# Front slots with the softmax shift ahead of the next normalisation, both filler matmuls in one place, one more front slot, and the fp8 and gate transposes one slot later

## What is computed

```python
x = x + _L0_xattn_ref(_layernorm(x, axis=-1), ctx_1024, ...)
x = x + _L0_ffn_ref(_layernorm(x, axis=-1), ...)      # six layers of local attention
x = x + _L1_xattn_ref(_layernorm(x, axis=-1), ctx_1024, ctx_1024, ...)
x = x + _L1_ffn_ref(_layernorm(x, axis=-1), L1_ffn_weight, L1_ffn_weight_scale, L1_ffn_bias)
x = x + _L2_xattn_ref(_layernorm(x, axis=-1), ctx_1024, ctx_1024, ...)
x = x + _L2_ffn_ref(_layernorm(x, axis=-1), ...)      # shared expert + top 2 of 8
x = x + _L3_xattn_ref(_layernorm(x, axis=-1), ctx_1024, ctx_1024, ...)
x = x + _L3_ffn_ref(_layernorm(x, axis=-1), ...)      # top 2 of 8 experts
```

## Time and profile before

| | |
|---|---|
| median of 3 runs | 2570.82 us (2570.54 to 2572.94) |
| the profiled execution's own time | 2574.15 us |
| its span | 2572.4 us |
| merged part, from the first `turn_x` to the end | 1734.8 to 2572.4 us |
| of it front slots 0 to 14, to the first expert matmul | 1734.8 to 1892.2 us |
| PE, DVE, ACT, POOL busy in the span | 2402.7, 1905.8, 1463.0, 1178.8 us |

### The profile page before, as it was taken

The page is one execution under the profiler, slowest core; times in us unless marked ns, Lnnn a source line. Parts: engine busy times, 40 slices in busy tenths (PEclk is TensorE's granted clock), DMA queues, the critical chain, the costliest instruction groups (busy, mean ns, idle before and its releaser), DMA issues.

```text
span 2572.4 us, 61077 instructions
## 1 busy us (share of the span) xinstructions
PE 2402.7 (93%) x25528; PEld 1452.4 (56%) x25528; DVE 1905.8 (74%) x3472; ACT 1463.0 (57%) x2051; POOL 1178.8 (46%) x867
## 2 busy tenths in 40 slices
PE   6887899999999999999999999977789999999999
PEld 5775566665666666566666566644444455554443
DVE  4765899999899999999999989935666666454322
ACT  2332566666666666666666666623356677665443
POOL 1221777767777777777776767711111111111000
PEclk9998999999999999999999999988899999999999
DMA  3000000100000000000000100002000001021111
GB/s 120 5 5 5 1 2 2 33 4 12 18 18 7 7 26 10 7 7 26 10 13 2 34 2 10 2 1 83 7 31 14 30 16 39 28 64 50 37 38 41
DMA packets 36006, 55.95 MB, mean 22 GB/s; under 512 B 6365, under 2 KB 20710, under 8 KB 35498
## 3 DMA queue, kind: packets, MB, share of 16 engines
q1 hardware_dynamic: 35754, 52.33, 6.6%
HBM read 51.13 MB, written 1.19 MB: 20 GB/s over the span
## 4 chain that ended last, share of the span: by engine, by line
PE 52%; DVE 25%; ACT 11%; issue 9%; POOL 3%; SPq 0%; DMA 0%; DVEq 0%; POOLq 0%; ACTq 0%
PE w L1402 9%; PE w L1412 8%; DVE turned L1056 4%; DVE norm L1063 4%; PE w L765 4%; PE w L790 4%; PE w L778 4%; PE py L803 4%; PE w L519 3%; DVE straight_odd L1051 2%; DVE top L568 2%; PE w L856 2%; ACT sq L1002 2%; PE w L1531 2%; ACT sq L993 2%
## 5 line engine op out<-in xcount | busy, mean ns | idle before, releaser
L593 POOL TENSOR_TENSOR prob<-prob,rden 128x1024 f32<-128x1024 f32 x112 | 213.2, 1904 | 207.5 <-DVE rden L582 207.5
L563 ACT ACTIVATE prob<-logit 128x512 f32<-128x512 f32 x224 | 137.6, 630 | 282.2 <-DVE logit L571 282.2
L1402 PE MATMUL w<-qT,m_fc 128*128 128x512 f32 x544 | 270.3, 609 | 0.0
L1172 POOL TENSOR_TENSOR straight_odd<-straight_odd,turned 128x1024 f32<-128x1024 f32 x96 | 227.3, 2368 | 82.8 <-DVE turned L1056 79.9
L1172 POOL TENSOR_TENSOR straight<-straight,turned 128x1024 f32<-128x1024 f32 x96 | 226.5, 2368 | 45.0 <-DVE turned L1056 45.0
L1056 DVE TENSOR_TENSOR turned<-w,rot 128x512 f32<-128x512 f32 x384 | 245.6, 681 | 0.0
L1166 POOL TENSOR_TENSOR straight_odd<-straight_odd,rnorms 128x1024 f32<-128x1024 f32 x96 | 180.6, 1902 | 116.9 <-DVE rnorms L1077 116.9
L1063 DVE TENSOR_REDUCE norm<-sq 128x16 f32<-128x1024 f32 x192 | 224.3, 1211 | 0.0
L1166 POOL TENSOR_TENSOR straight<-straight,rnorms 128x1024 f32<-128x1024 f32 x96 | 180.5, 1900 | 72.4 <-DVE rnorms L1077 72.4
L611 POOL TENSOR_TENSOR fresh_roots<-fresh_means,eps 128x1 f32<-128x1 f32 x64 | 12.1, 190 | 401.2 <-DVE fresh_means L600 401.2
L765 PE MATMUL w<-b_wqkv,m_proj 128*128 128x512 f32 x384 | 192.8, 625 | 2.8 <-DVE turned L1056 1.5
(11 more groups left out here) (259 smaller groups left out, 5270.0 us busy)
## 6 DMA issues: line engine op xcount, KB each, us to landing
b_wqkv<-gates SPq DMA_DIRECT2D x64, 256.0 KB, 3.7
b_wqkv<-in_b_wqkv SPq DMA_DIRECT2D x18, 512.0 KB, 3.6
ctxT<-in_ctxT SPq DMA_DIRECT2D x64, 64.0 KB, 1.8
...
```

Of the source, the lines that this page charges most:

```text
L593: pool.tensor_tensor(flat, flat, k.rden[:, s, :, None].broadcast_to([P, HEADS, SEQ]), ALU.mult).then_inc(k.prob_ready, 1)
L1172: pool.tensor_tensor(k.straights[s][:, i, :, :], k.straights[s][:, i, :, :], k.turned[:, i, :, :], ALU.add).then_inc(added, 1)
L1402: pe.matmul(claim(("hidden", J, c)), k.m_fc[:, x, c * P:(c + 1) * P], k.m_xT[:, q, :], start=True, stop=True).then_inc(k.ring_full, 1)
```

## The change

1. `LEAD` is 16 instead of 15, so there are 16 front slots, and 86 slots instead of 85.
2. In front slots VectorE does `shift` ahead of the next work's `normalise`, which comes ahead of `scale_rows`. Slots with jobs keep their order.
3. In front slots both filler matmuls stand behind `queries`; none stands behind `rows`.
4. `turn_quantised` moves from the end of the quantising slot into the next (in front slots behind `queries`, in slots with jobs behind the second `hidden`), the product to the end of that slot, and `add_product` to the beginning of the slot after it.
5. The works' slots are given one by one. L1's tile 8 takes slot 8, quads of L2 and L3 begin one slot later than before, and slot 24 has no work.
6. Gates are turned, stored and spread one slot after they are made (`GATES_TURN_AT`). Counted from the start of a block of jobs, the transposes, logits and gates of every block but the first stand one slot or two earlier, as the table says; the gates' transposes stand behind `queries`.
7. `normalise_vector` is a `scalar_tensor_tensor` whose second tensor is the inverse root broadcast along the row, instead of a `tensor_scalar` with two scalars per partition.

```diff
 def normalise_vector(dve, k, n, T, s, rows, to):
     dve.wait_ge(n.rstd, T + 1)
-    return dve.tensor_scalar(to, rows, n.means[:, s, 0:1], n.roots[:, s, :], ALU.subtract, ALU.mult)
+    return dve.scalar_tensor_tensor(out=to, in0=rows, scalar=n.means[:, s, 0:1], in1=n.roots[:, s, :].broadcast_to([P, P]),
+                                    op0=ALU.subtract, op1=ALU.mult)
...
-LEAD = 15
+LEAD = 16
...
-QUAD_START = {(0, 0): 0, (0, 1): 4, (1, 0): 8, (1, 1): 12, (0, 2): 16, (0, 3): 20, (1, 2): 24, (1, 3): 28,
-              (2, 0): 32, (2, 1): 36, (2, 2): 45, (2, 3): 54}
-WORKS = sorted((first + j, n, 4 * q + j) for (n, q), first in QUAD_START.items() for j in range(4))
+WORK_SLOTS = {(0, 0): (0, 1, 2, 3), (0, 1): (4, 5, 6, 7), (0, 2): (8, 17, 18, 19), (0, 3): (20, 21, 22, 23),
+              (1, 0): (9, 10, 11, 12), (1, 1): (13, 14, 15, 16), (1, 2): (25, 26, 27, 28), (1, 3): (29, 30, 31, 32),
...
-QUANTISE_AT = {QUAD_START[0, q] + 6: q for q in range(QUADS)}
+QUANTISE_AT = {WORK_SLOTS[0, q][3] + 3: q for q in range(QUADS)}
 PRODUCT_AT = {u + 1: q for u, q in QUANTISE_AT.items()}
...
-TURN_AT = {block(e, q) - (3 if e else 1): (e, q) for e, q in BLOCKS}
-RAW_AT = {block(1, q) - 3: q for q in range(QUADS)}
-LOGITS_AT = {block(e, q) - (2 if e else 1): (e, q) for e, q in BLOCKS}
-GATES_AT = {block(e, q) - e: (e, q) for e, q in BLOCKS}
+FIRST_BLOCK = (0, 0)
+TURN_AT = {block(e, q) - (1 if (e, q) == FIRST_BLOCK else 3 + e): (e, q) for e, q in BLOCKS}
+RAW_AT = {block(1, q) - 4: q for q in range(QUADS)}
+LOGITS_AT = {block(e, q) - (1 if (e, q) == FIRST_BLOCK else 2 + e): (e, q) for e, q in BLOCKS}
+GATES_AT = {block(e, q) - (0 if (e, q) == FIRST_BLOCK else 1 + e): (e, q) for e, q in BLOCKS}
+GATES_TURN_AT = {u + 1: block_of for u, block_of in GATES_AT.items()}
...
@@ front_slot
             values(work[0], work[2], u)
             queries(work[0], work[2])
+        if u in PRODUCT_AT:
+            turn_quantised(PRODUCT_AT[u])
+        occupy()
         occupy()
...
             rows(before2[0], before2[2], u)
-        occupy()
...
@@ slots with jobs, TensorE
             if job:
                 hidden(job, 1)
+            if u in PRODUCT_AT:
+                turn_quantised(PRODUCT_AT[u])
...
+            if u in GATES_TURN_AT:
+                gates(*GATES_TURN_AT[u])
...
@@ merged_vector
-        if u in PRODUCT_AT:
-            add_product(PRODUCT_AT[u])
+        if u - 1 in PRODUCT_AT:
+            add_product(PRODUCT_AT[u - 1])
         if after:
             stats(*after)
+        if after and u >= LEAD:
             normalise(after[1], after[2])
         if before2 and u >= LEAD:
             scale_rows(before2[2], u)
         if before:
             shift(before[2])
+        if after and u < LEAD:
+            normalise(after[1], after[2])
         if before2 and u < LEAD:
             scale_rows(before2[2], u)
```

More of the change, by code:

```diff
@@ L1278 @@
 SPREAD = 6
-QUAD_START = {(0, 0): 0, (0, 1): 4, (1, 0): 8, (1, 1): 12, (0, 2): 16, (0, 3): 20, (1, 2): 24, (1, 3): 28,
-              (2, 0): 32, (2, 1): 36, (2, 2): 45, (2, 3): 54}
-WORKS = sorted((first + j, n, 4 * q + j) for (n, q), first in QUAD_START.items() for j in range(4))
+WORK_SLOTS = {(0, 0): (0, 1, 2, 3), (0, 1): (4, 5, 6, 7), (0, 2): (8, 17, 18, 19), (0, 3): (20, 21, 22, 23),
+              (1, 0): (9, 10, 11, 12), (1, 1): (13, 14, 15, 16), (1, 2): (25, 26, 27, 28), (1, 3): (29, 30, 31, 32),
+              (2, 0): (33, 34, 35, 36), (2, 1): (37, 38, 39, 40), (2, 2): (46, 47, 48, 49), (2, 3): (55, 56, 57, 58)}
+WORKS = sorted((slot, n, 4 * q + j) for (n, q), slots in WORK_SLOTS.items() for j, slot in enumerate(slots))
 WORK_AT = {u: (n, t, W) for W, (u, n, t) in enumerate(WORKS)}
 NUMBER = {(n, t): W for n, t, W in WORK_AT.values()}
-QUANTISE_AT = {QUAD_START[0, q] + 6: q for q in range(QUADS)}
+QUANTISE_AT = {WORK_SLOTS[0, q][3] + 3: q for q in range(QUADS)}
 PRODUCT_AT = {u + 1: q for u, q in QUANTISE_AT.items()}
@@ L1326, in ring_uses @@
     for u in range(SLOTS):
+        job = [("hidden", job_at(u)[4], c) for c in range(4)] if job_at(u) else []
+        uses += [(u, use) for use in job[0:2]]
+        if u in PRODUCT_AT:
+            uses.append((u, ("quantised", PRODUCT_AT[u])))
+        uses += [(u, use) for use in job[2:4]]
+        if u in GATES_TURN_AT:
+            uses.append((u, ("gates",) + GATES_TURN_AT[u]))
+        if u in TURN_AT:
+            uses.append((u, ("turn",) + TURN_AT[u]))
         if u in PRODUCT_AT:
             uses.append((u, ("product", PRODUCT_AT[u])))
-        if job_at(u):
-            uses += [(u, ("hidden", job_at(u)[4], c)) for c in range(4)]
-        if u in TURN_AT:
-            uses.append((u, ("turn",) + TURN_AT[u]))
         if u in RAW_AT:
@@ L1580, in merged_tensor @@
         job, last = job_at(u), job_at(u - 1)
-        if u in PRODUCT_AT:
-            product(PRODUCT_AT[u])
         if u < LEAD:
@@ L1622, in merged_tensor @@
                 turn_probs(before[2])
+        if u in PRODUCT_AT:
+            product(PRODUCT_AT[u])
         if u in RAW_AT:
@@ L1626, in merged_tensor @@
             logits(*LOGITS_AT[u])
-        if u in GATES_AT:
-            gates(*GATES_AT[u])
         if u == SIM_AT:
             sim()
-        if u in QUANTISE_AT:
-            turn_quantised(QUANTISE_AT[u])
 def merged_scalar(act, k):
@@ L1679, in turned_probs, with turned_quantised @@
         act.copy(k.probT[:, :, :], logits_bank(k, W)[:, :]).then_inc(d.pT_ready, 1)
+    def turned_quantised(q):
+        turned = full(("quantised", q))[:, 0:256].bitcast(BF16)
+        act.copy(k.f_qT[:, :, :], turned).then_inc(k.ring_read, 1)
     def quad_exp(e, q):
@@ L1693, in merged_scalar @@
         job = job_at(u)
-        if u in PRODUCT_AT:
-            q = PRODUCT_AT[u]
-            act.wait_ge(k.f.done, q)
-            act.copy(k.f_prod, full(("product", q))).then_inc(k.ring_read, 1)
         if job:
@@ L1703, in merged_scalar @@
             gelu(job, 1)
+        if u in PRODUCT_AT and u >= LEAD:
+            turned_quantised(PRODUCT_AT[u])
+        if job:
             gelu(job, 2)
@@ L1717, in merged_scalar @@
                 turned_probs(before[2])
+        if u in GATES_TURN_AT:
+            e, q = GATES_TURN_AT[u]
+            act.copy(k.m_gateT[0:NE[e], 512 * q:512 * q + 512], full(("gates", e, q))[0:NE[e], :]).then_inc(k.ring_read, 1)
         if u in TURN_AT:
@@ L1728, in merged_scalar @@
             turned_probs(before[2])
+        if u in PRODUCT_AT:
+            q = PRODUCT_AT[u]
+            act.wait_ge(k.f.done, q)
+            act.copy(k.f_prod, full(("product", q))).then_inc(k.ring_read, 1)
         if u in RAW_AT:
@@ L1736, in merged_scalar @@
             act.copy(k.m_raw[:, 0:n], full(("logits", e, q))[:, 0:n]).then_inc(k.ring_read, 1)
-        if u in GATES_AT:
-            e, q = GATES_AT[u]
-            act.copy(k.m_gateT[0:NE[e], 512 * q:512 * q + 512], full(("gates", e, q))[0:NE[e], :]).then_inc(k.ring_read, 1)
         if u == SIM_AT:
             act.copy(k.m_simT[:, :], full(("sim", 1, 0))[:, 0:8]).then_inc(k.ring_read, 1)
-        if u in QUANTISE_AT:
-            turned = full(("quantised", QUANTISE_AT[u]))[:, 0:256].bitcast(BF16)
-            act.copy(k.f_qT[:, :, :], turned).then_inc(k.ring_read, 1)
 def merged_vector(dve, k):
@@ L1988, in reload @@
         sp.dma_start(k.m_proj[:, x, :, :], a["m3_proj"][:, x, :, :]).then_inc(k.e3_weights, 16)
+    spread_at = {block_of: u for u, block_of in GATES_TURN_AT.items()}
     gated = [job_at(u)[4] for u in range(SLOTS) if job_at(u) and job_at(u)[2] < 8]
@@ L2008, in merged_sync @@
             free = LEAD + gated[g - SPREAD] + 2 if g >= SPREAD else 0
-            if u == max(block(e, q) - e, free):
+            if u == max(spread_at[e, q], free):
                 spread(J)
```

15 lines of the change are left out of this document (7 added, 8 removed).

## The result

| | before | after |
|---|---|---|
| median | 2571.88 us of 4 (2570.54 to 2573.97) | 2534.66 us of 4 (2530.97 to 2535.23) |
| ratio of after to before | | 0.985, 95% interval 0.9836 to 0.9863 |
| the profiled execution's own time, its span | 2574.15, 2572.4 us | 2534.94, 2533.2 us |
| first `turn_x` | 1734.81 | 1732.79 |
| front, to the first expert matmul | 157.38 us | 135.74 us |

The changed kernel is 37.2 us faster; 33 us were forecast, and the predicted time of 2538 us is 3.3 us above the median. The two profiles differ by 39.2 us of span: 21.6 in the front, 15.5 behind it, and 2.0 ahead of the first `turn_x`, where only the normalisation's form was changed.

What follows compares the result with a forecast made beforehand. Front bound by a chain over VectorE, ScalarE and TensorE, slots 17 to 21 by TensorE. Terms -22.1 - 4.1 - 6.5 - 0.3 = -33.0 us from 2574.15 gave 2541.2, as median 2538 us; range 2527 to 2555.

Steps and rivals of the forecast that it cites:

- The chain: Front slots: `shift` ahead of `normalise` takes a 1.00 us wait and 0.26 us off the chain, -1.26 us a slot.
- The form: Normalisation in front slots: as `scalar_tensor_tensor` it escapes the slowdown beside GpSimd's bias addition, -0.12 us a slot, else 0.
- The clock: Ordinary front slots: TensorE 87% busy in 7.64 us keeps the clock at its upper level; bound 1.1 us a slot.
- A: Rival: the clock still falls in most front slots, 14 us given back, about 2552 us; chance 0.14.
- C: Rival: two fillers at 1.2 GHz become the front's bound, slots of 12.0 us, about 2595 us; chance 0.05.
- Ends and quantising: Front: -1.5 us for slot 1, 2.6 instead of 3.4 us at the end, 6.9 us added for each of two quantisings.
- Work moved to the front: Slots 24 to 26: one work fewer beside jobs, net -4.1 us.
- Quantising beside jobs: Slots 22, 23, 26, 27: later transposes leave 3.5 us of stall against 6.8 and 7.4, -6.5 us for both.
- Gates: Other blocks: only TensorE's wait for gates goes, -0.3 us; 1.0 us for slots 24 and 25 counted with moved work.
- B: Rival: only the front gains and the second half, beside jobs, gives nothing, about 2549 us; chance 0.08.
- D: Rival: in front slots `top` finds its scores late, about 2568 us; chance 0.03.

Runs made afterwards that it cites:

- b_shift: Kernel before with only `shift` put ahead of `normalise` on VectorE in front slots: 2552.27 us, ratio 0.9926.
- b_fill: Kernel before with only both front-slot fillers put together behind `queries`: 2569.41 us, ratio 0.9994.
- a_no_fill: Changed kernel without any filler matmuls in front slots: 2560.28 us, ratio 0.9949 to the kernel before.
- a_bias_late: Changed kernel with normalisation as `tensor_scalar` again and GpSimd adding the bias behind the second root instead of ahead: 2532.16 us.
- a_best: Changed kernel with slots 20 and 25 workless instead of 24, `tensor_scalar` again, GpSimd's bias behind its root, last two quantising instructions in the next slot: 2528.20 us.
- a_holes: Changed kernel with slots 20 and 25 without work instead of 24, each two slots ahead of a quantising slot: 2530.74 us.
- a_form_back: Changed kernel with only the normalisation as `tensor_scalar` again: 2536.28 us, ratio 0.9852 to the kernel before.
- a_gates_back: Changed kernel with the gates' transposes and copy back in the slot where VectorE makes the gates: 2538.97 us.
- a_load_26: Changed kernel with three VectorE maxima that change nothing added in slot 26 ahead of the quantising: 2539.65 us.

## Why the prediction was right, step by step

**The chain (right).** The 1.26 us a slot are there: 9.02 to 7.74 in b_shift, with the old form and the fillers where they were. In the changed kernel 7.81 us stand against 7.64 forecast, and the front gained 21.6 us against 22.1.

**The form (wrong sign).** Forecast -0.12 us a slot, "0 if not"; measured 471 to 538 ns, +0.07. The step that failed is the choice between the bounds: the earlier trace rows show 346 ns in 16 cases, but none beside GpSimd's addition, as the text itself said, and that was the one condition that counted. The bound of nothing was too good as well. By the Trainium skill (VectorE: DVE Perf Modes, section "Mode 2×_2P — use both read ports for one tensor") the old form handles two fp32 elements a cycle and one with a second tensor handles one, from which the prediction estimated 0.07 us more for each. The sign and size came out, but not by that reason: away from the addition the old form takes 335 to 348 ns and the new one 341 to 353, as the rows had shown.

**The clock (right outcome, one of two reasons wrong).** It stays at 1.00 in ordinary front slots, so rivals A (2552) and C (2595) are out. Against A I credited the filled idle time. But b_shift leaves a filler at each end of the slot, TensorE still waits 0.97 us ahead of `turn_rows`, and it has 1.00 too; and in b_fill, with the fillers in one place, the clock falls: in a slot of 9.02 us with 6.66 us of work TensorE idles 2.4 us wherever they stand. The other ground of the prediction, the same work in a shorter slot, is what the runs bear out: slots of 7.74 us, with 6.75 us of work, keep the clock in b_shift, and slots without the fillers' part of that work don't in a_no_fill. What C describes, fillers at 1.2 GHz that hold up `turn_rows`, does happen, but only in the slot behind each quantising (3.78 us for the two).

**Ends and quantising (right, within 1 us, in part by luck).** Slots 0 to 2 gave 2.5 us instead of 1.5, the end 1.2 instead of 0.8. Slots 7 and 8 are 13.51 + 8.99 - 2 x 7.81 = 6.9 us over two ordinary ones, as forecast; the other pair 6.6. The parts are not those of the sum, though: it leaves the fillers out of that slot's path. They are as late there as VectorE: the scaled rows are ready 0.2 us ahead of `turn_rows` in a_bias_late, 1.2 us in a_best.

**Work moved to the front (about right).** The forecast of 4.1 us net is for slots 24 to 26. Slots 24 and 25 went from 24.87 to 21.65 us, 3.2 us; slot 26's share is a tile's third stage, about 1.2 us by slot 22 of a_holes. That makes 4.4.

**Quantising beside jobs (one of two mis-sized).** For slots 22 and 23 the sum was 6.8 - 3.5 - 0.35 = 3.0 us, measured 3.0, which is in part luck: a_form_back and a_gates_back have 27.1 us there instead of 28.8, a gain of 4.7. The surviving stall is there, but it is not `turn_rows` that waits: TensorE waits 2.16 us for the rounded rows, and the rest is a lower clock behind (0.94). `s_rows` is ready 1.9 us ahead of `turn_rows`; in slot 23 VectorE has no next work to normalise ahead of it, which I take to be why. For slots 26 and 27 the same sum gave 3.55 us, and 7.3 were measured, of which about 1.2 are slot 26's share above: 6.1 are left. The step that failed is "the next `apply` starts 4.8 us behind the slot's start": it took the quantising's place in the slot from the earlier trace rows, though the table of works empties slot 26's third stage, and in slot 27 `apply` starts 1.6 us behind. a_load_26 and a_holes show that this is the cause. Where VectorE is late and a next work is there, slot 27 of a_load_26, the stall is the one of the sum: 2.68 + 0.81 = 3.5 us, most of it at the transposes.

**Gates (too small).** Forecast -0.3 for blocks outside slots 24 and 25 and 1.0 within the term for the moved work, measured 4.3 us (5.7 by the ratios) in a_gates_back. The profiles, which differ by 2.9 us, have 0.5 us of wait and 1.7 of clock in the first block and about 2 us from slot 29 on, with waits of 0.4 to 0.7 us in four later slots. The term that was too small is "only the wait for the gates goes", 0.3 us for all other blocks together, where three slots outside 24 and 25 have 1.8 us of such waits. Of the kernel's gain behind the front, 1.7 us lie in the first two slots with jobs, 13.66 and 11.55 us before, 11.61 and 11.91 now; the four kernels made from the one before have 13.4 to 14.7 us in the first, and five of those made from the changed one 12.8 to 13.8 us. So these 1.7 us can't be put down to one edit.

**B and D** are out: the second half gained 15.5 us, and in the front `top` waits for no scores.

The sum: the front 0.5 us less than forecast, the part with jobs 15.5 instead of 10.9, and 2.0 ahead of it.

Left open: which of the two levels of the clock a slot gets after the same idle time (slots 16 and 17 of a_form_back against those of the changed kernel; slots 12 and 13 of the kernel before), how much of the gates' gain is clock, and the first 2 us.
